# Layer 0 weight lookup on one Trainium2 core: sixteen terms as seven operands in place of ten, in units 1 to 5

## The reference, cut to what matters

```
x = x + 0.5 * _L0_ffn_ref(_layernorm(x, axis=-1), L0_ffn_lut, L0_ffn_gate_idx, L0_ffn_up_idx, L0_ffn_down_idx)

def _ghost_linear(x, idx, lut):
    w = lut[idx]
    return jnp.einsum('bsh,oh->bso', x, w)
```

## Time and profile before

| quantity | value |
|---|---|
| median of 3 runs | 2323.51 us (2321.5 to 2327.88) |
| the profiled execution's own time | 2320.97 us |
| its span | 2319.2 us |
| granted TensorE clock, mean over the span | 0.905 |
| TensorE matmuls busy | 1939.5 us (84% of the span) |
| VectorE busy | 1214.6 us (52%) |
| ScalarE busy | 836.5 us (36%) |
| the stage of the change: from the first lookup to the last write of x | 22.34 to 166.54 us of the span |

### The profile page before, as it was taken

How to read it: one execution, slowest core, us unless ns; L and a number is a source line. 1 busy time by engine, 2 the same in 40 slices (tenths; PEclk the granted TensorE clock), 3 DMA queues, 4 the chain that set the end, 5 groups by cost and what they waited for, 6 DMA issues and landing times. The chain is left out here.

```text
span 2319.2 us, 52385 instructions
## 1 busy us (share of the span) xinstructions
PE 1939.5 (84%) x21291; PEld 1337.0 (58%) x21293; DVE 1214.6 (52%) x3220; ACT 836.5 (36%) x1973; POOL 459.6 (20%) x536
## 2 busy tenths in 40 slices
PE   7994779997999996676899999999999797779568
PEld 3542654565677664454666676666666674546445
DVE  6657542434465335734566566666666227552541
ACT  1012321221453222232666657666665202220120
POOL 0002320232000322551221122122121003710200
PEclk9997989997999997786999999999999798799679
DMA  4000000341500425752001001000100217730000
GB/s 160 0 0 14 1 5 1 121 180 47 218 1 4 128 83 167 242 195 82 30 21 40 21 21 40 21 21 24 37 21 21 65 33 238 239 134 2 9 7 19
DMA packets 55235, 157.39 MB, mean 68 GB/s; under 512 B 12803, under 2 KB 29785, under 8 KB 50726
## 3 DMA queue, kind: packets, MB, share of 16 engines
q1 hardware_dynamic: 45110, 128.84, 16.7%
q0 software_dynamic: 9888, 25.20, 3.3%
HBM read 115.36 MB, written 40.48 MB: 67 GB/s over the span
## 5 line engine op out<-in xcount | busy, mean ns | idle before, releaser
L2247 PE MATMUL l_heads_ps_p<-xnT,l2a_w 128*128 128x512 f32 x512 | 253.5, 620 | 8.6 <-DMA l2a_w<-in_l_w_heads 8.6
L2647 DVE SCALAR_TENSOR_TENSOR l_heads_taps<-l_heads_padded,l_heads_conv,l_heads_taps 128x1024 f32<-128x1024 f32 x144 | 183.7, 1286 | 8.2 <-ACT l_heads_taps L2473 7.5
L2247 PEld LDWEIGHTS l_heads_ps_p<-xnT,l2a_w 128*128 128x128 f32 x512 | 88.4, 191 | 79.9 <-issue 63.2
L206 PE MATMUL norm_turn<-zeros,ident 128*128 128x512 f32 x120 | 66.1, 707 | 53.9 <-PEq L60 53.9
L2822 POOL TENSOR_TENSOR l_heads_e<-l2a_table,l_heads_row 128x512 f32<-128x512 f32 x32 | 33.3, 1042 | 389.9 <-DVE l_heads_first L2658 384.5
L197 ACT ACT_TABLE_LOAD x10 | 12.8, 1283 | 217.9 <-PEq L60 217.9
L379 PE MATMUL l_ffn_a_ps_w<-l_ffn_a_term,ident 128*128 128x512 f32 x240 | 76.7, 473 | 8.9 <-DVE l_ffn_a_term L477 8.9
L578 POOL TENSOR_TENSOR l_qkv_by_sin<-l_qkv_raw,l_qkv_angle 128x512 f32<-128x512 f32 (+1 forms) x16 | 23.2, 1451 | 284.0 <-ACT l_qkv_raw L566 280.6
L206 PEld LDWEIGHTS norm_turn<-zeros,ident 128*128 128x128 f32 x120 | 26.1, 226 | 88.2 <-issue 88.2
L2473 ACT ACTIVATE l_heads_taps<-l_heads_ps_p,l_heads_conv 128x512 f32<-128x512 f32 x96 | 76.0, 792 | 0.0
L2472 ACT COPY l_heads_padded<-l_heads_ps_p 128x512 f32<-128x512 f32 x96 | 56.5, 589 | 52.5 <-PE l_heads_ps_p L2247 52.5
(11 more groups left out here) (697 smaller groups left out, 4924.6 us busy)
## 6 DMA issues: line engine op xcount, KB each, us to landing
l_results<-zeros SPq DMA_DIRECT2D x24, 512.0 KB, 6.2
l_ffn_a_w_in<-in_l_in_w SPq DMA_DIRECT2D x8, 1536.0 KB, 10.7
l_ffn_b_w_in<-in_l_in_w SPq DMA_DIRECT2D x8, 1536.0 KB, 9.5
l2a_w<-in_l_w_heads SPq DMA_DIRECT2D x16, 512.0 KB, 3.7
l_heads_row<-l_rows SPq DMA_DIRECT2D x16, 512.0 KB, 4.8
l_ffn_a_w_out<-in_l_out_w SPq DMA_DIRECT2D x8, 768.0 KB, 8.5
l_ffn_a_w_in<-l_results SPq DMA_DIRECT2D x8, 768.0 KB, 6.5
l_ffn_b_w_out<-in_l_out_w SPq DMA_DIRECT2D x8, 768.0 KB, 8.4
```

Source lines behind the costliest of these rows:

```text
L206: pe.matmul(turn[:, i % KC, (i // KC) % HALVES, :], core.ident[:], core.zeros[:, 0:HALF], start=True, stop=True)
L2247: mm = pe.matmul(ps_p[half][:], w[b][:, which, c, :], core.xnT[:, c, half * HALF:(half + 1) * HALF], start=(c == 0), stop=(c == KC - 1))
L2647: dve.scalar_tensor_tensor(out=taps[which][:], in0=padded[which][:, :, j:j + SEQ], scalar=conv[p % 2][:, which, j:j + 1], in1=taps[which][ ...
```

## The change

Unit 0 keeps its ten operands. Units 1 to 5 get seven: five pairs and two triples. A triple is made of three lookups and two adds, both into the term's slot: the first add raises a new semaphore `added`, and the second waits for it and for the third lookup. The three parts of a unit's decode now hold 3, 2 and 2 operands. `upto(u)` counts the operands of the units before u, since they no longer all have the same number. The spare tile still alternates between two, and a lookup into it waits for the sum before the last, whichever semaphore that one raised (`sums_made`).

```diff
-    OPERANDS = ((0, 1), (2,), (3, 4), (5,), (6, 7), (8,), (9, 10), (11,), (12, 13), (14, 15))
-    PARTS = (range(0, 4), range(4, 7), range(7, 10))
-    COUNT = len(OPERANDS)
+    FIRST = ((0, 1), (2,), (3, 4), (5,), (6, 7), (8,), (9, 10), (11,), (12, 13), (14, 15))
+    OTHERS = ((0, 1), (2, 3, 4), (5, 6), (7, 8, 9), (10, 11), (12, 13), (14, 15))
     SLOTS = 5
+    def operands(u):
+        return OTHERS if u else FIRST
+    def upto(u):
+        return len(FIRST) + (u - 1) * len(OTHERS) if u else 0
+    def parts_of(u):
+        return (range(0, 3), range(3, 5), range(5, 7)) if u else (range(0, 4), range(4, 7), range(7, 10))
...
-                for m in PARTS[part]:
-                    n = u * COUNT + m
+                for m in parts_of(u)[part]:
+                    n = upto(u) + m
...
-                                       start=(m == 0), stop=(m == COUNT - 1))
+                                       start=(m == 0), stop=(m == len(operands(u)) - 1))
...
-                        first, other = OPERANDS[m]
-                        spare = second[len(paired) % 2]
-                        look_up(u, first, slot[:])
-                        if len(paired) >= 2:
-                            dve.wait_ge(term_ready, paired[-2])
-                        look_up(u, other, spare[:])
-                        dve.wait_ge(looked_up, lookups[0])
-                        dve.tensor_tensor(slot[:], slot[:], spare[:], ALU.add).then_inc(term_ready, 1)
-                        paired.append(n + 1)
+                    look_up(u, entries[0], slot[:])
+                    for j in entries[1:]:
+                        spare = second[len(sums_made) % 2]
+                        if len(sums_made) >= 2:
+                            dve.wait_ge(*sums_made[-2])
+                        look_up(u, j, spare[:])
+                        dve.wait_ge(looked_up, lookups[0])
+                        if j != entries[1]:
+                            dve.wait_ge(*sums_made[-1])
+                        if j == entries[-1]:
+                            dve.tensor_tensor(slot[:], slot[:], spare[:], ALU.add).then_inc(term_ready, 1)
+                            sums_made.append((term_ready, n + 1))
+                        else:
+                            dve.tensor_tensor(slot[:], slot[:], spare[:], ALU.add).then_inc(added, 1)
+                            inner[0] += 1
+                            sums_made.append((added, inner[0]))
```

More of the change, by code:

```diff
@@ L346, in l0_decode_ffn_stage @@
         term_summed = st.sem("term_summed")
+        added = st.sem("added")
         w_ready = st.sem("w_ready")
@@ L400, in down @@
                 mm.then_inc(down_done, 1)
-            for part in range(len(PARTS)):
+            for part in range(3):
                 decode(0, part)
@@ L429, in keep @@
             def keep(u):
-                act.wait_ge(term_summed, COUNT * (u + 1))
+                act.wait_ge(term_summed, upto(u + 1))
                 for bank, at in zip(ps_w, columns):
@@ L449, in _ @@
             lookups = [0]
-            paired = []
+            inner = [0]
+            sums_made = []
             def look_up(u, j, out):
@@ L464, in make_terms @@
                         dve.wait_ge(term_summed, n - SLOTS + 1)
-                    if len(OPERANDS[m]) == 1:
-                        dve.tensor_scalar(slot[:], idx[:, u, :], float(OPERANDS[m][0]),
-                                          table[:, OPERANDS[m][0]:OPERANDS[m][0] + 1], ALU.is_equal, ALU.mult)\
+                    entries = operands(u)[m]
+                    if len(entries) == 1:
+                        j = entries[0]
+                        dve.tensor_scalar(slot[:], idx[:, u, :], float(j), table[:, j:j + 1], ALU.is_equal, ALU.mult)\
                             .then_inc(term_ready, 1)
-                    else:
-                        first, other = OPERANDS[m]
-                        spare = second[len(paired) % 2]
-                        look_up(u, first, slot[:])
-                        if len(paired) >= 2:
-                            dve.wait_ge(term_ready, paired[-2])
-                        look_up(u, other, spare[:])
-                        dve.wait_ge(looked_up, lookups[0])
-                        dve.tensor_tensor(slot[:], slot[:], spare[:], ALU.add).then_inc(term_ready, 1)
-                        paired.append(n + 1)
+                        continue
+                    look_up(u, entries[0], slot[:])
[4 more added lines that the diff above has]
+                        look_up(u, j, spare[:])
+                        dve.wait_ge(looked_up, lookups[0])
+                        if j != entries[1]:
[7 more added lines that the diff above has]
+                            sums_made.append((added, inner[0]))
             def mix(u, h):
```

## The result

The changed kernel takes 2303.12 us (median of 17 runs), the kernel before beside it 2320.52 us (median of 17). The ratio is 0.9927, with a 95% interval of 0.9913 to 0.9940: 0.73% faster. The medians differ by 17.4 us, and the interval stands for 14 to 20 us. One of the 17 executions of the kernel before took 3301.92 us, far outside all the others, and is left out of the ratio. The profiled execution has a span of 2301.4 us, 17.8 less than before.

What follows compares the result with a forecast made beforehand. TensorE was taken to pace five rounds of 22.34 us; 3.61 us removed from each, less a new wait of 0.21, gave 17.0 us in all, from the median 2323.51 to 2306.5 us, range 2301.5 to 2312.

Steps and rivals of the forecast that it cites:

- The bound: Between unit 0's decode and unit 5's products, TensorE sets the pace, at 22.34 us a round.
- The removal: Three operands fewer on TensorE in each of five rounds: 3.61 us a round, 18.05 us in all.
- The added work: Three more VectorE adds a unit; a triple costs 3.38 us, VectorE's round goes from 14.86 to 17.68 us.
- the second semaphore: In a triple's second add, the wait for `added`, long raised by then, was priced at nothing.
- The new wait: TensorE stands 0.21 us once a round at operand 6, whose sum comes late from VectorE.
- VectorE's own wait at mix(u,1): VectorE, ahead of its third part, stands 1.12 us a round at mix(u,1).
- The sum: Five rounds of 18.94 us, each 3.40 us less than before, give 17.0 us.
- VectorE as the pace: Rival in the five rounds: VectorE paces at 19.9 us a round, kernel at 2311.3 us; chance 0.06.
- The clock did not fall: Answers a rival: TensorE's clock falls from standing once a round, kernel slower, 2343.9 us with two rounds; chance 0.03.
- the rest gives the gain back: Rival: later stages' cold starts give most of the 17 us back, or measurement hides it, about 2318 us; chance 0.06.
- the first rival: VectorE becomes the pace if no instruction overlaps the one ahead: gain 12.2 us, 2311.3 us; chance 0.06.

Runs made afterwards that it cites:

- the removal alone: The changed kernel with table entries 4 and 9 left out in units 1 to 5, so seven pairs without triples; ratio 0.9892 against before.
- the pair ahead of the mix: The changed kernel with VectorE making operand 5 before mix(u,1), TensorE's order the same; ratio 0.9898 against before.
- the change's two traces: The changed kernel profiled twice, nothing altered the second time; the second run's ratio against before was 0.9917.
- the four traces shown: Traces of the kernel before, the changed kernel twice, and the changed kernel with operand 5 made before mix(u,1); 2152.7, 2151.1, 2147.9 and 2160.5 us behind the stage.

## Why the prediction was right

**The bound.** TensorE set the pace of the five rounds and still does, at 18.97 us in 22.34. Shown from both sides: the removal alone gives rounds of 18.97 us, and three more adds on VectorE leave the rounds of 22.34 as they are.

**The removal.** 3.61 us a round was said. Without the wait the round is 18.73 us (the pair ahead of the mix), so it is 3.61.

**The added work.** A triple was put at 3.38 us from a pair's rows and took 3.39; the second semaphore, taken at nothing, cost 0.01 us at most.

**The new wait.** 0.21 us at the last operand of each round was said, and it was 0.24, at that place, in all five. Its cause as walked, silu, mix and two pairs, holds: it stays when VectorE has less to do and goes when one pair moves ahead of the mix. VectorE's own wait at mix(u,1) was said to be 1.1 us and was 1.02.

**The sum.** Five rounds were to give 17.0 us and gave 111.79 - 94.92 = 16.87 (39.43 to 151.22 and 40.09 to 135.01, starts of up(0,0) and up(5,0)). The stage ended at 150.32 us and not at 149.5, in the main because up(0,0) started 0.66 us later in that execution: 0.31 us since the stage began later, and 0.35 since TensorE's clock came up later in unit 0 (0.87 from 28 to 32 us, against 0.99 before). The medians moved by 17.4 us. That this is so near 17.0 is in part luck, as the interval is 14 to 20 us; what bears the sum out is the 16.87 us of the traces. The predicted 2306.5 us was 3.4 above the time measured, 3.0 of which is the lower median of before in the larger set of runs.

**The rivals.** VectorE as the pace begins one operand further down, at six. The clock did not fall in the rounds of the change; it fell with four operands, behind standing of 2.53 us, and there in two rounds of five. That the rest gives the gain back is not borne out: the part behind the stage was 1.6 and 4.8 us shorter than before in the change's two traces, less than the 12.6 us over which the four traces shown spread.

**Short stands and overlap.** For 0.24 us once a round, and for 0.39 to 1.26 us three times a round, the traces show no fall of the clock. The Trainium skill, page "TensorE: Matmul & The Clock Gate", section "A second HAM failure mode: psum-queue depth-cycling", warns of short idle spells that make the clock oscillate; with stands of these lengths the traces do not show it, with those of four operands they show a clock that falls and comes back. Lookups of 0.586 us that start every 0.50 us speak against the first rival in the changed kernel too. The Trainium skill, page "VectorE: DVE Perf Modes", section "The DRAIN you can't avoid", says that a next op does not start until the pipe is empty, which gives that rival when read strictly.

## What to carry to other kernels

Where two engines share a sum, write down what one operand costs each of them, here 1.20 us of TensorE against 0.94 us of VectorE, and move operands until the two rounds meet; past that point the other engine paces, and each further operand moved makes the round longer. Here the rounds are 18.97 us with seven operands, 18.63 with six, where VectorE has become the pace, and 19.57 with five: the shortest is six, one step beyond the change. Equal sums are not enough: walk the order of the engine that works in order, since one that stands at a wait early in the round may be late at its end, and moving one operand across that wait can repair it. Judge such a change by the length of the rounds in the trace where the runs of a whole kernel vary by more than the gain, and count a part of the program without the other engine's cover (here unit 0) for itself.

## What the runs showed of the hardware

- GpSimd's add of 128 x 716 in float32 took 1.97 us, where its 1.04 us for 128 x 512 let me expect 1.46, and a VectorE lookup that started beside it stood for most of it (2.02 us for 0.586). A lookup of VectorE's was still running for the first 0.42 us of the add (79.91 + 0.58 = 80.49, from 80.07); if the add stood for these, 1.55 us are left, an estimate, as no run shows the add alone. Handing VectorE's work to an idle GpSimd lost time: rounds of 20.03 us, against 18.63.
- A granted clock of 1.00 outlived standing of 1.26 us in each round with five operands, and of 2.53 us in three rounds with four, but not in the fourth and fifth. There it fell to 0.50 only after TensorE had been at work again for about 1 us, and down(3,1) took 3.39 us for 1.72.
- In unit 0, with TensorE standing between operands (seven operands there too), the clock came up later: 0.50 from 28 to 32 us and 0.85 from 32 to 36. The change's second trace, in which TensorE's first matmul starts at the same time (25.39 and 25.38 us), has 0.75 and 1.00, its first trace 0.87 and 1.00. That the standing is the cause rests on one trace.
